# Four graph layers on one core: the building of the counts written out without loops, with constant addresses and waits

## What is computed

```python
edge_index = jnp.stack([src, dst])
x = _layernorm(x + _L0_gnn_ref(x, edge_index, ...))               # GCN, twice gcn_conv
x = _layernorm(x + _L1_gnn_ref(x, edge_index, ...))               # GAT, 4 heads
x = _layernorm(x + _L2_gnn_ref(x, edge_index, edge_weight, ...))  # weighted attention, 8 heads
x = _layernorm(x + _L3_gnn_ref(x, edge_index, ...))               # GAT, 4 heads, and a feed-forward part

# gcn_conv: what bears on this change
norm = dinv[src] * dinv[dst]
msg = xw[src] * norm[:, None]
out = jax.ops.segment_sum(msg, dst, num_segments=n)
```

## Time and profile before

| what | value |
|---|---|
| median of 3 runs | 4278.55 us (4275.5 to 4282.44) |
| the profiled execution | 4277.48 us, its span 4275.7 us |
| busy share of the span | PE 66%, PEld 43%, DVE 73%, ACT 56%, POOL 67% |
| mean granted TensorE clock | 0.841 |
| the stage that is changed | from 138.6 us of the span to about 718 us |

### The profile page before, as it was taken

One profiled execution on the slowest core, in us unless ns is written; L12 is line 12 of the kernel. 1 busy time (PEld: TensorE's weight loads), 2 busy tenths in 40 slices (PEclk: granted clock), 3 DMA queues, 4 the chain that ended last, 5 costly groups with the idle time before them and its releaser, 6 DMA issues. The chain is left out here.

```text
span 4275.7 us, 61386 instructions
## 1 busy us (share of the span) xinstructions
PE 2828.8 (66%) x16208; PEld 1819.7 (43%) x16208; DVE 3116.2 (73%) x9331; ACT 2391.8 (56%) x5229; POOL 2872.2 (67%) x3193
## 2 busy tenths in 40 slices
PE   1698888994567676676256776767625666676763
PEld 1344444552345444454234444535423444454542
DVE  5999997555467777678747786877874777686785
ACT  0677775003556666664356665656545666665644
POOL 5799994202777777773477777777437777777743
PEclk8899999996788888897578887888867888897886
DMA  3011111451232333231133333233103323232220
GB/s 102 28 82 81 58 78 81 167 216 47 64 69 68 69 68 69 69 69 43 32 69 70 70 70 70 66 70 70 41 22 73 69 68 69 69 69 68 64 51 15
DMA packets 127618, 298.41 MB, mean 70 GB/s; under 512 B 45412, under 2 KB 74972, under 8 KB 123712
## 3 DMA queue, kind: packets, MB, share of 16 engines
q0 software_dynamic: 74976, 155.58, 16.6%
q1 hardware_dynamic: 52320, 139.24, 9.7%
HBM read 241.28 MB, written 53.38 MB: 69 GB/s over the span
## 5 line engine op out<-in xcount | busy, mean ns | idle before, releaser
L1411 POOL DMA_INDIRECT work<-table,lane_src x2184 | 2092.5, 958 | 665.6 <-issue 643.7
L1508 PE MATMUL psum<-work 128*128 128x396 bf16 (+1 forms) x5850 | 1165.0, 355 | 68.1 <-ACT work L1453 34.4
L1450 ACT ACTIVATE work<-work,middle_node_number 128x384 f16<-128x384 f16 x1587 | 954.3, 601 | 225.1 <-PE psum L1508 202.8
L1453 ACT ACTIVATE work<-work 128x384 bf16<-128x384 f16 x1587 | 829.6, 523 | 50.5
L1565 PE MATMUL psum<-work 128*128 128x136 f32 x4836 | 701.2, 304 | 188.9 <-DVE work L1696 96.5
L1508 PEld LDWEIGHTS psum<-work 128*128 128x128 bf16 x5850 | 598.2, 104 | 513.8 <-issue 122.5
L1565 PEld LDWEIGHTS psum<-work 128*128 128x128 f32 x4836 | 654.6, 209 | 273.7 <-issue 160.6
L1733 DVE TENSOR_TENSOR node_sums<-node_sums,psum 128x136 f32 x2418 | 558.1, 293 | 103.1 <-PE psum L1565 96.2
L767 POOL TENSOR_SCALAR work<-work 128x128 f16<-128x128 f16 x784 | 540.7, 708 | 74.9 <-POOLq L663 60.2
L745 DVE TENSOR_SCALAR work<-work 128x400 f16<-128x400 f16 x1568 | 484.9, 351 | 6.4 <-PEq L663 3.6
L716 PE MATMUL psum<-work 128*128 128x448 f16 x2100 | 456.1, 355 | 3.2 <-PEq L1131 2.5
(11 more groups left out here) (361 smaller groups left out, 2852.8 us busy)
## 6 DMA issues: line engine op xcount, KB each, us to landing
counts<-work SPq DMA_DIRECT2D x14, 2800.0 KB, 9.3
work<-counts SPq DMA_DIRECT2D x14, 2800.0 KB, 10.2
work<-table,lane_src POOLq DMA_INDIRECT x2184, 2.6
work<-spread SPq DMA_DIRECT2D x78, 256.0 KB, 4.0
work<-masks SPq DMA_DIRECT2D x78, 128.0 KB, 3.0
work<-source_rows SPq DMA_DIRECT2D x39, 192.0 KB, 3.8
spread<-node_sums SPq DMA_DIRECT2D x4, 896.0 KB
table<-work SPq DMA_DIRECT2D x10, 330.0 KB, 3.0
```

Source lines behind the costliest of these rows:

```text
L1411: pool.indirect_dma_start(m.ring[:, s % SLOTS, 0:F + H], None, m.d_table[H], bass.IndirectOffsetOnAxis(ap=m.src[:, s:s + 1], axis=0)).then ...
L1450: act.activation(away, rows_of(g, u), ACT.Abs, bias=m.low_tile[:, hi:hi + 1]).then_inc(far_known, 1)
L1453: act.activation(hot_of(g, u), away, ACT.Relu, bias=1.0, scale=-1.0).then_inc(hot_act, 1)
L1508: mm = pe.matmul(aid_banks[:, k, 0:3 * (F + H)], hot_of(g, u)[:, k * P:(k + 1) * P], m.all_thirds[:, :, hi, 0:F + H], start=(hi == 0), sto ...
```

## The change

The three compute loops become Python loops: each engine's program is written out for all 14 chunks. `n` and `c` are then plain numbers, so `bass.ds(n, 1)` becomes `n:n + 1`, waits have constant values, and the guards of the first units become plain comparisons. The places of the sums (`j_regs`) still come from registers, loaded once for each chunk. No operation, no order, no buffer and no semaphore changes. The whole diff:

```diff
 def take_sum(dve, m, n0, k, q, summed):
     if k % CREGS == 0:
-        dve.load(m.j_regs, m.cj_row[0:1, bass.ds(n0 + k, CREGS)])
+        dve.load(m.j_regs, m.cj_row[0:1, n0 + k:n0 + k + CREGS])
     j = dve.snap(m.j_regs[k % CREGS], min_val=0, max_val=NPAD)
-    if not (isinstance(n0, int) and n0 + k < 2):
+    if n0 + k >= 2:
         dve.wait_ge(summed, n0 + (k - 1))
...
# vector
-                    if not (isinstance(n, int) and n < DEPTH):
+                    if n >= DEPTH:
                         dve.wait_ge(unit_done, n - (DEPTH - 1))
...
-                            dve.tensor_scalar(m.hot_lo[:, d, b, :], m.iota_cols[:, 0:P], m.low[:, b, bass.ds(n, 1)], None, ALU.is_equal)
-                        t = dve.tensor_scalar(m.hot_key[:, d, b, :], m.iota_cols[:], m.key[:, b, bass.ds(n, 1)], None, ALU.is_equal)
+                            dve.tensor_scalar(m.hot_lo[:, d, b, :], m.iota_cols[:, 0:P], m.low[:, b, n:n + 1], None, ALU.is_equal)
+                        t = dve.tensor_scalar(m.hot_key[:, d, b, :], m.iota_cols[:], m.key[:, b, n:n + 1], None, ALU.is_equal)
...
             for c in range(4):
                 chunk(c, c % 2, c // 2)
-            with dve.Fori(2, CHUNKS // 2) as i:
+            for i in range(2, CHUNKS // 2):
                 chunk(i * 2, 0, i)
                 chunk(i * 2 + 1, 1, i)
# tensor
-                first = isinstance(c, int) and c == 0
...
-                    if not (isinstance(n, int) and n < 4):
+                    if n >= 4:
                         pe.wait_ge(evacuated, n - 3)
...
-            with pe.Fori(1, CHUNKS // 2) as i:
+            for i in range(1, CHUNKS // 2):
# scalar
-                act.activation(away, m.iota_cols[:, 0:P], ACT.Abs, bias=m.low_last[:, bass.ds(n, 1)], scale=-1.0).then_inc(lo_away, 1)
+                act.activation(away, m.iota_cols[:, 0:P], ACT.Abs, bias=m.low_last[:, n:n + 1], scale=-1.0).then_inc(lo_away, 1)
...
-            with act.Fori(1, CHUNKS // 2) as i:
+            for i in range(1, CHUNKS // 2):
```

More of the change, by code:

```diff
@@ L743, in chunk @@
                         if PAIRED <= b < CB - 1:
-                            dve.tensor_scalar(m.hot_lo[:, d, b, :], m.iota_cols[:, 0:P], m.low[:, b, bass.ds(n, 1)], None, ALU.is_equal)
-                        t = dve.tensor_scalar(m.hot_key[:, d, b, :], m.iota_cols[:], m.key[:, b, bass.ds(n, 1)], None, ALU.is_equal)
+                            dve.tensor_scalar(m.hot_lo[:, d, b, :], m.iota_cols[:, 0:P], m.low[:, b, n:n + 1], None, ALU.is_equal)
+                        t = dve.tensor_scalar(m.hot_key[:, d, b, :], m.iota_cols[:], m.key[:, b, n:n + 1], None, ALU.is_equal)
                     t.then_inc(hot, 1)
-                    if not (isinstance(c, int) and c < 2):
+                    if c >= 2:
                         if k == 0:
@@ L784, in chunk @@
                     t.then_inc(unit_done, 1)
-                    if not first and k < NODE_TILES:
-                        if k == 0 and not (isinstance(c, int) and c < 3):
+                    if c and k < NODE_TILES:
+                        if k == 0 and c >= 3:
                             pe.wait_ge(summed, (c - 2) * CHUNK)
```

## The result

| | before | changed |
|---|---|---|
| median of 10 runs each | 4275.24 us (4271.92 to 4282.44) | 4265.81 us (4261.81 to 4271.53) |
| the profiled execution: time, span | 4277.48, 4275.7 | 4271.53, 4269.7 |
| mean granted TensorE clock | 0.841 | 0.841 |

The ratio is 0.9977, 95% interval [0.9968, 0.9987]: 9.4 us faster, between 5.6 and 13.7. The forecast was 4265 us and a gain of 13.3. That the time came within 1 us is partly luck: the forecast started from the median of three runs, 4278.55 us, and the median of ten is 3.3 us lower, while the gain came out 3.9 us smaller. The profiled execution of the changed kernel is the slowest of its ten, so the two spans differ by only 6.0 us; the stage has to be read by itself.

What follows compares the result with a forecast made beforehand. DVE and POOL together were taken to bound the stage, with a hole at each DVE jump. Only the jumps' 13.3 us counted, other terms 0: 4278.55 - 13.3 = 4265.2 us, predicted 4265, range 4259 to 4273.

Steps and rivals of the forecast that it cites:

- (b): DVE's four jumps back go: 13.3 us net gained, bounds 12 to 14.8.
- Jump and load: DVE's loop top: a 3.1 us jump eats the sequencer's 2.5 us lead, leaving the register load open, up to 3.86 us.
- (a): DVE's register addresses and waits go: 0, at most 1 us either way.
- (c): PE's and ACT's five jumps back go: 0, hidden by the four one-hot buffers.
- (d): POOL, already written out: its 14.7 us of waits not added; its slower rate is already in 1.392 us a unit.
- (f): Fetching more sequential instructions on three engines: taken as 0, at most 7 us over ten chunks.
- The load's hole at even chunks: Rival, DVE before L710: the holes are the load's, 12.2 us stay, only 2.6 go; 4276 us; chance 0.06.
- POOL gave the time back: Rival denied this: DVE and POOL settle slower without holes, four iterations keep 325 us; 4278 us; chance 0.05.
- sequences didn't starve: Rival on DVE: written-out code starves sequencers, 3.1 us in each of ten chunks; 4296 us; chance 0.05.

Runs made afterwards that it cites:

- turned loop: Kernel before with DVE's loop begun mid-chunk (unit 14), so no register load stands behind its three jumps: 5788.19 us against 5799.92, ratio 0.9974; stage 570.50 us.
- first two groups: Follow-ups on two slower chips: loops written out separately, one jump or a shifted loop (before: 5799.92 us); then repeats and added PE matmuls (before: 5795.61 us).

## Why the prediction was right

**(b) The jumps.** Confirmed by place and number: DVE's jumps alone, four of them, two holes each. Predicted 13.3 us net; the loop's part measures 13.2 us, the stage 12.6. The 0.6 us between are in the tail, which I took to move as a whole: from the last unit's sum to the hidden layer it took 718.96 - 694.25 = 24.7 us before and 706.83 - 681.58 = 25.25 after. That is about half of why L1194 (now L1193) started at 706.83 us and not at 705.7; most of the rest is that the stage began 0.5 us later in this execution. That the gain stays under the 14.8 us of idle time, since POOL's rest had let DVE hurry, held as well.

**Jump and load.** The reading that the jump eats the lead, and that the load then lies open, is what the turned loop shows: three short holes behind the jumps, no other. The reading was incomplete in one point. I had taken the load's length of up to 3.86 us as something that comes with a jump; it comes with the store of the counts, which the late load runs into. The four loads together take 13.7 us in place of 4 x 1.85 = 7.4, so some 6.3 of the 14.8 us of idle time are the store's (an estimate from the loads' lengths). The forecast did not need the cause, for it took the lost time as measured at this place; with 64 more instructions in front the same edit would have been worth some 30 us (an estimate, 597.46 - 567.75).

**(a), (c), (d), (f): nothing.** Chunks stay at 39.0 us with and without register addresses; PE's and ACT's jumps cost nothing; POOL keeps its 0.696 us a one-hot with its rests gone; no fetch shows in the written-out code. The rule on sequential prefetch in the Trainium skill ("Runtime: NRT & Kernel Launch", "Instruction fetch mechanics") agrees with what the traces show: ten chunks in sequence without a hole, and a price only at a taken branch. The estimate of 5.6 us for a load, from the same section's 200 ns a register, fell: the section names uncached AXI and not HBM, and here a load takes 66 ns a register unless a store lies over it.

**The rivals.** The load's hole at even chunks didn't stay; POOL gave the time back; sequences didn't starve. The gain over the whole time, 9.4 us with an interval from 5.6 to 13.7, holds the stage's 12.6 and, barely, the forecast's 13.3.

## What to carry to other kernels

In this stage a hardware loop costs at its jump and nowhere else: look for "issue" idle time of an engine once in each iteration, and multiply by the jumps of the engine that sets the pace; the loops of the others could stay. What stands first in the body matters more than the jump, so before writing a loop out, turn it so that plain work stands at its top and a register load far behind it; the turned loop alone won 9.9 of the 12.6 us here, of which one jump fewer is some 3. Look also at what DMA runs while a late register load is open: here a store out of SBUF made it one and a half to over three times as long. And do not carry over the price of a jump from another program, for it was 0.9, 3.2 or 7.4 us in kernels that do the same work.

## What the runs showed of the hardware

- A load of 28 registers from SBUF takes 1.85 us, 66 ns a register, and is hidden as long as the sequencer leads. Under a DMA store out of SBUF the same load took 2.7 to 6.1 us (24 loads in seven traces), under DMA loads into SBUF at most 1.89.
- From a jump back in DVE's loop to the sequencer's next instruction it takes 2.8 to 3.2 us in seven traces, and 3.5 to 3.8 with 64 empty instructions put in front.
- POOL's 128x128 one-hot takes 597 ns next to an idle DVE, 696 ns on average with two of them in a unit (39.0 / 56), and 827 ns when DVE has six one-hots in each unit.
- The two chips of the first two groups ran this stage at the same pace to 0.1%, but the whole program in 5.80 ms in place of 4.28: the later stages waited more (in the kernel with DVE's loop alone written out, POOL's gathers waited 690 us for PE's L1565 between 1100 and 4100 us). The mean granted clock was 0.754 in place of 0.841. What was slow there wasn't looked into; it stays open.
